# Second layer of a two-layer model on one core: the inverse roots of eight norms by Newton steps on VectorE, with the layer's four written orders made anew

## What is computed

```
x = x + L1_attn_a(layernorm(x))   # a linear layer, sigmoid and tanh, a linear scan over the tokens
x = x + L1_ffn(layernorm(x))      # silu(h @ up) * (h @ gate) @ down, ternary weights, 1024 wide
x = x + L1_attn_b(layernorm(x))   # rmsnorm, a gated linear recurrence (RG-LRU), rmsnorm, a gelu MLP 768 wide
x = x + L1_ffn(layernorm(x))      # the same feed-forward block again
```

## Time and profile before

| | |
|---|---|
| median of 3 runs | 1489.52 us (1486.73 to 1493.4) |
| the profiled execution | 1492.75 us, of which the span from the first to the last instruction is 1491.5 us |
| PE busy | 1424.5 us, 96% of the span |
| DVE, ACT, POOL busy | 1078.2, 1045.0, 678.5 us |
| second layer | 1224.5 to 1491.5 us of the span, 267 us |
| ACT_TABLE_LOAD in the second layer | 42, of 1283 ns each |

### The profile page before, as it was taken

How to read it: one execution, slowest core, us unless ns; L and a number is a source line. 1 busy time by engine, 2 the same in 40 slices (tenths; PEclk the granted TensorE clock), 3 DMA queues, 4 the chain that set the end, 5 groups by cost and what they waited for, 6 DMA issues and landing times.

```text
span 1491.5 us, 23534 instructions
## 1 busy us (share of the span) xinstructions
PE 1424.5 (96%) x8388; PEld 1215.6 (81%) x8388; DVE 1078.2 (72%) x2439; ACT 1045.0 (70%) x2281; POOL 678.5 (45%) x822
## 2 busy tenths in 40 slices
PE   7899999999999998998999999999999998979899
PEld 6789898888989886786898888888897786656677
DVE  6989898989898985656776666666676748567534
ACT  4898989999898987474665555655564646584754
POOL 6676776676767546113433343333321111822223
PEclk9999999999999999898999999999999999998999
DMA  2000000000000000601000000000001404000000
GB/s 74 2 18 1 19 9 12 1 19 19 1 8 2 15 1 1 268 1 51 22 15 15 22 23 14 22 22 22 1 8 63 207 28 171 1 1 1 1 0 29
DMA packets 14339, 45.11 MB, mean 30 GB/s; under 512 B 3216, under 2 KB 3216, under 8 KB 12048
## 3 DMA queue, kind: packets, MB, share of 16 engines
q1 hardware_dynamic: 14224, 43.61, 8.1%
HBM read 42.55 MB, written 1.05 MB: 29 GB/s over the span
## 4 chain that ended last, share of the span: by engine, by line
PE 75%; DVE 15%; ACT 7%; issue 1%; POOL 1%; DVEq 0%; ACTq 0%; POOLq 0%
PE ps L149 32%; PE ps L355 15%; PE ps L344 10%; PE ps L1198 6%; DVE a_pT_lo L411 3%; PE ps L2007 3%; PE ps L2013 2%; DVE a_prob L364 2%; DVE a_q L694 1%; PE ps L2023 1%; PE ps L2009 1%; PE ps L2026 1%; PE ps L1910 1%; PE ps L614 1%; ACT a_prob L371 1%
## 5 line engine op out<-in xcount | busy, mean ns | idle before, releaser
L386 POOL TENSOR_SCALAR a_prob<-a_prob,a_rowinv 128x128 f32<-128x128 f32 (+7 forms) x256 | 188.2, 749 | 132.8 <-DVE a_rowinv L380 132.7
L411 DVE TENSOR_TENSOR a_pT_lo<-ps,a_pT_hi 128x512 fp32r<-128x512 f32 (+3 forms) x384 | 194.7, 551 | 21.1 <-ACT a_pT_hi L403 19.4
L364 DVE CUSTOM_DVE_ANT_0 a_prob<-ps,a_mask 128x128 f32<-128x128 f32 (+7 forms) x256 | 187.1, 750 | 21.2 <-PE ps L149 20.9
L371 ACT ACTIVATE a_prob<-a_prob,a_negmax 128x128 f32<-128x128 f32 (+7 forms) x256 | 197.3, 778 | 2.2 <-DVE a_negmax L364 1.3
L386 POOL TENSOR_SCALAR b_prob<-b_prob,b_rowinv 128x128 f32<-128x128 f32 (+7 forms) x128 | 94.3, 748 | 199.9 <-DVE b_rowinv L380 199.8
L403 ACT ACTIVATE a_pT_hi<-ps 128x512 fp32r<-128x512 f32 (+3 forms) x384 | 167.2, 492 | 24.7 <-PE ps L344 15.6
L344 PE MATMUL ps<-ident,a_prob 128*128 128x128 f32 x1152 | 160.2, 275 | 7.1 <-DVE a_pT_lo L411 5.7
L371 ACT ACTIVATE b_prob<-b_prob,b_negmax 128x128 f32<-128x128 f32 (+7 forms) x128 | 99.6, 779 | 72.6 <-DVE b_negmax L364 71.8
L344 PEld LDWEIGHTS ps<-ident,a_prob 128*128 128x128 f32 x1152 | 130.0, 140 | 20.6 <-POOL a_prob L386 8.0
L149 PE MATMUL ps<-a_k_hi,a_q 128*128 128x512 f32 (+3 forms) x384 | 140.4, 373 | 1.8 <-DVE a_negmax L364 1.2
L355 PE MATMUL ps<-a_pT_hi,a_v 128*128 128x512 f32 (+3 forms) x384 | 131.1, 349 | 1.1 <-DVE a_pT_lo L411 0.6
(11 more groups left out here) (457 smaller groups left out, 4024.0 us busy)
## 6 DMA issues: line engine op xcount, KB each, us to landing
f_wq<-in_f_wq SPq DMA_DIRECT2D x2, 2048.0 KB, 8.9
f_wo<-in_f_wo SPq DMA_DIRECT2D x2, 2048.0 KB, 17.1
b_w_raw<-in_b_qk SPq DMA_DIRECT2D x16, 256.0 KB, 2.6
a_w_raw<-in_a_w SPq DMA_DIRECT2D x8, 384.0 KB, 3.2
a_vo<-in_a_o SPq DMA_DIRECT2D x8, 256.0 KB, 2.7
f_wk<-in_f_wk SPq DMA_DIRECT2D x2, 1024.0 KB, 10.8
f_wv<-in_f_wv SPq DMA_DIRECT2D x2, 1024.0 KB, 12.8
f_wg<-in_f_wg SPq DMA_DIRECT2D x2, 1024.0 KB, 19.7
```

Source lines behind the costliest of these rows:

```text
L364: dve.tensor_tensor_reduce(slot(a, u), g.ps_flat[:, bank * HALF:bank * HALF + width], a.mask[:, N - width:], -1.0, -MASKED, ALU.add, ALU.m ...
L371: act.activation(prob, prob, ACT.Exp, bias=a.negmax[:, n:n + 1], scale=-1.0, accum_out=a.rowsum[:, n:n + 1]).then_inc(*g.exped.mark(a.tag, u))
L386: pool.tensor_scalar(prob, prob, a.rowinv[:, n:n + 1], 1.0, ALU.mult, ALU.mult).then_inc(*g.normed.mark(a.tag, u))
L411: dve.tensor_tensor(lo, src, fr(hi), ALU.subtract).then_inc(*g.lo.mark(a.tag, u, j0 // 4))
```

## The change

Three things change, all in the second layer.

1. **ACT loses its root in eight norms** (r, t1, n2, t2 of both halves): `half_root_act` is no longer called there, and with it go the 128x4 ACTIVATE and the table loads around it. The listing of ACT's order has 32 ACT_TABLE_LOAD in the layer now, 42 before.
2. **DVE computes the inverse root itself**, from the variance in PSUM: add eps, shift the bits right by one, subtract them from a constant (a first guess), and three Newton steps of three instructions each, `half_inverse_dve`. That is 12 instructions on 128x4 values in place of one reciprocal. Each waits for the one before it by a semaphore. The product inside a Newton step is kept in PSUM, in four unused columns of `q.bank[1]`.
3. **All four order strings are new.** The steps are the same ones (ACT has eight fewer), in another interleaving of prep, half 0 and half 1.

```diff
+ROOT_BITS, ROOT_STEPS = float(0x5F375A00), 3
+I32 = mybir.dt.int32
 L1_PE = (
-    "12112201201112122110211121211111112111112111112211121222122112211112222211112222211221121112122122122112222111111122"
...
+    "12112012101112210221211112111121111111111111221111222212121211122221222111122222211122121112122222211122212111111112"
...
-def half_inverse_dve(g, dve, q, tag):
-    dve.wait_ge(*q.act.at(tag, "std"))
-    dve.reciprocal(q.inv[:], q.std[:]).then_inc(*q.dve.mark(tag, "rec"))
+def half_inverse_dve(g, dve, q, tag, eps):
+
+    done, part = q.dve, q.bank[1][:, HT:2 * HT]
+    dve.wait_ge(*q.pe.at(tag, "var"))
+    dve.tensor_scalar(q.std[:], q.bank[1][:, 0:HT], eps, None, ALU.add).then_inc(*done.mark(tag, "plus"))
+    dve.wait_ge(*done.at(tag, "plus"))
+    dve.tensor_scalar(q.inv[:].bitcast(I32), q.std[:].bitcast(I32), 1, None, ALU.logical_shift_right).then_inc(*done.mark(tag, "half_bits"))
+    dve.wait_ge(*done.at(tag, "half_bits"))
+    dve.tensor_scalar(q.inv[:].bitcast(I32), q.inv[:].bitcast(I32), -1.0, ROOT_BITS, ALU.mult, ALU.add).then_inc(*done.mark(tag, "step", 0))
+    for n in range(ROOT_STEPS):
+        dve.wait_ge(*done.at(tag, "step", n))
+        dve.tensor_tensor(part, q.inv[:], q.inv[:], ALU.mult).then_inc(*done.mark(tag, "part", n))
+        dve.wait_ge(*done.at(tag, "part", n))
+        dve.scalar_tensor_tensor(part, part, -0.5, q.std[:], ALU.mult, ALU.mult).then_inc(*done.mark(tag, "slope", n))
+        dve.wait_ge(*done.at(tag, "slope", n))
+        event = (tag, "rec") if n == ROOT_STEPS - 1 else (tag, "step", n + 1)
+        dve.scalar_tensor_tensor(q.inv[:], part, 1.5, q.inv[:], ALU.add, ALU.mult).then_inc(*done.mark(*event))
     yield
...
-def half_norm_act(g, act, q, tag, eps):
+def half_norm_act(g, act, q, tag):
     yield from half_square_act(g, act, q, tag, q.h, "cen")
-    yield from half_root_act(g, act, q, tag, eps)
     yield from half_hi_act(act, q, tag, q.h, "out")
...
     yield from half_square_act(g, act, q, "n2", q.u, "x1")
-    yield from half_root_act(g, act, q, "n2", 1e-8)
     yield from half_hi_act(act, q, "n2", q.h, "out")
```

More of the change, by code:

```diff
@@ L1688 @@
 RING = 3
+ROOT_BITS, ROOT_STEPS = float(0x5F375A00), 3
+I32 = mybir.dt.int32
 L1_PE = (
[L1690 to L1691 removed]
+    "12112012101112210221211112111121111111111111221111222212121211122221222111122222211122121112122222211122212111111112"
+    "21212122222222122221221121122212111111211111211122122122222222222222222111222")
 L1_DVE = (
[L1693 to L1694 removed]
+    "01112212112101000002121202110010102201121120012012112210011221111211211121111111121212111111121111121121122111122212"
+    "22222222212222112222122222222121211222222111221211111222212212112122221222221122211222")
 L1_ACT = (
[L1696 to L1697 removed]
+    "11220110111122112020221112211111111011221111212211112211221222211121111111211221121111222222112221122211222221122211"
+    "221222222112222211122211112211111112122112222222221222222")
 L1_POOL = (
[L1699 removed]
+    "0110101011010022222201112011212111222222211111112222222")
 def by_turns(order, *programs):
@@ L1988, in half_norm_dve @@
     yield from half_squares_dve(dve, q, tag)
-    yield from half_inverse_dve(g, dve, q, tag)
+    yield from half_inverse_dve(g, dve, q, tag, 1e-5)
     dve.wait_ge(*q.pe.at(tag, "inv"))
@@ L2110, in half_act @@
 def half_act(g, l, act, q):
-    yield from half_norm_act(g, act, q, "r", 1e-5)
+    yield from half_norm_act(g, act, q, "r")
     for n, m in enumerate((0, 2, 1, 3)):
@@ L2127, in half_ternary_act @@
 def half_ternary_act(g, l, act, q, tag):
-    yield from half_norm_act(g, act, q, tag, 1e-5)
+    yield from half_norm_act(g, act, q, tag)
     for f in range(TE_T):
@@ L2294, in half_lru_dve @@
     yield from half_squares_dve(dve, q, "n2")
-    yield from half_inverse_dve(g, dve, q, "n2")
+    yield from half_inverse_dve(g, dve, q, "n2", 1e-8)
     dve.wait_ge(*pe.at("n2", "inv"))
```

6 lines of the change are left out of this document (removed).

## The result

The changed kernel takes **1500.88 us** in the median of 5 runs (1496.38 to 1506.11) against 1489.52 us for the kernel before: a ratio of 1.0073, 95% interval 1.0055 to 1.0091. It is 11 us slower. The forecast was 1498 us, with 1483 to 1505 as its range.

The account below looks back on a forecast made before the run. The prediction took PE, busy 96% of the span, to bound the kernel. Stretch terms 0.5 + 0 + 7.0 + 1.7 - 0.7 = +8.5 gave 1501.2 us profiled, less 3.2 for the median: 1498 us, range 1483 to 1505.

Parts of the forecast that it names:

- The turns: DVE and POOL alternate by operation; five SBUF-only instructions of the twelve each wait up to one POOL operation; 9.3 us.
- The walk through n2 of half 0: Fourth stretch: remainder, sum of squares, shift and subtraction wait for POOL's operations in turn; +7.7 us, taken as +7.0.
- the longer chain: n2 of half 0: twelve dependent DVE instructions delay the spread even without turns, 5.75 instead of 3.9 us, +1.9.
- The order terms: First two stretches: new interleaving costs +2.0 us in the first; the second, with its other terms, is taken as -3.8.
- The second stretch: To half 0's l mean: moved blocks, less idle and slow clock, against turns in t1 of half 1; -3.8 us taken.
- The third stretch: To the end of half 0's `out`: the silu cut goes (3.3 us), ga starts some 3 us later; 0, give or take 2.
- The fifth stretch: To half 1's n2 spread: order nearly the same, 2.35 us chain faces one 1.4 us down block, adds come behind; +1.7 us.
- The sixth stretch: To the end: blocks of 4.7 to 5.6 us cover the chain in t2's norms; tail stays; -0.7 us.
- The last step: From the profiled 1501.2 us to the median: subtract 3.2 us, as the profiled execution before stood over its median; 1498.
- the turns don't bite: Rival, no change: four elements too few for the second port, or splits fall elsewhere; 9.3 us go, 1489; chance 0.27.
- ScalarE's relief decides: Rival, faster: removed ACT table loads and the uncut ga free more than the rows name; -8.4 us, 1481; chance 0.17.
- the clock decides: Rival, slower: longer norm in n2 of half 0 starves PE and lowers its clock; 1501 to 1507 us; chance 0.13.

Follow-up runs that it names:

- e4: Changed kernel with the same twelve instructions, but variance plus eps and shifted bits kept in PSUM, so none reads SBUF alone: 1490.11 us, ratio 1.0000.
- e10: Changed kernel with POOL's two long weight-remainder subtractions cut, r_lo into four pieces and down_lo into six, same work: 1497.62 us, ratio 1.0057.
- e3: Changed kernel with POOL's split of the down weights and half 1's last remainder moved ahead of both adds to x: 1502.09 us, ratio 1.0078.
- e6: e4's chain in PSUM with the order strings of the kernel before: 1503.82 us, ratio 1.0095.
- e12: e4 with the old order on all four engines from half 0's l mean to its n2 spread (third and fourth stretch): 1493.76 us, ratio 1.0020.
- e1: Kernel before with the four new order strings, keeping ScalarE's root and its eight steps: 1494.80 us, ratio 1.0026.
- e2: Changed kernel (Newton root on DVE, chain in SBUF) with the four old order strings, less ScalarE's eight root steps: 1508.77 us, ratio 1.0128.

## Why the prediction was right, step by step

| stretch | forecast | measured |
|---|---|---|
| 1, to t1's first block | +4.3 | +3.7 |
| 2, to half 0's l mean | -3.8 | -3.8 |
| 3, to the end of `out` | 0 | -0.6 |
| 4, to the spread of n2, half 0 | +7.0 | +7.9 |
| 5, to the spread of n2, half 1 | +1.7 | +3.2 |
| 6, to the end | -0.7 | -1.9 |
| sum | +8.5 | +8.5 |

**The turns** are shown, by e4 (taken away), e10 (their size changed) and e3 (moved). In r of half 0 one instruction took 2.08 us, where about 2.2 was expected; in n2 of half 0 the gap between variance and spread is 6.65 us, where 5 or more was to prove the turns. In the sum they were 2.3 + 1.9 + 5.1 = 9.3 us; taking those of the twelve away is worth 10.8 in the median and 8.4 in the stretches. The Trainium skill (SBUF — State Buffer, Who interferes with whom) says that a VectorE instruction with two SBUF inputs, or in a two-port mode, blocks against a POOL operation that reads SBUF, and that one with at most one SBUF input outside those modes does not. The runs agree for the squarings, which wait in the changed kernel, and for e4, where none of the twelve waits. Shift and subtraction have one SBUF input and wait as well; that they ran in a two-port mode is not shown, since the profile does not name the mode. That the shift and the subtraction on 128x4 count, which the prediction had left open, is shown by their 2.08 and 3.32 us.

**The walk through n2 of half 0** came out at 12.9 us against a forecast of 12.0 (5.0 + 7.0), but not by its own steps. The remainder did not wait for POOL (0.68 us at 1347.65), and the shift ran free (0.17), since the long split began only 0.04 us after it. The subtraction waited for the long split and the squaring for the add, one place later each than I wrote.

Its terms were off by more than its result. I had 1.9 us for the longer chain and 5.1 for turns, and nothing for the order. The table splits the 7.9 otherwise. From e4 to the changed kernel it is 3.2, the turns of the twelve; with the turn of the sum of squares, which e4 keeps (1.57 us in place of 0.69), it is 4.1. The other 4.7 (9.7 less 5.0) are there without any turn in the chain. By e6, which has the long chain in the old order and reads 6.9, 1.9 of them are the chain and 2.8 the order, which I had left out: it puts the two down rounds behind the variance, PE's wait of 3.11 us for the sum of squares has nothing to cover it, and what follows runs at half clock. How chain and order share the 4.7 is not settled, since e12, whose order there is e6's, reads 8.2 at a granted clock of 0.87 where e6 has 0.99. That the turns fell short of my term and the rest went over it by about as much is luck.

**The order terms.** In the first stretch I had 2.3 for the turn in r and 2.0 for the order, a walk. PE's wait for that spread gives the turn: 2.18 us in the changed kernel, 0.26 in e4.

```profile
1232.58 1.16 PE L249 MATMUL ps<-ident,l_inv 128*128 128x128 f32 x8 [2.18 <-DVE l_inv L1985]
```

```profile
1233.03 1.16 PE L249 MATMUL ps<-ident,l_inv 128*128 128x128 f32 x8 [0.26 <-DVE l_inv L1985]
```

That leaves 1.8 of the +3.7 for the order and the longer chain, and e4's first stretch is 1.7 over before (42.3 less 40.6), within the 2 us that such a stretch varies. e1's +3.6 does not speak against it: it has no chain, but PE waits 2.75 us for x ahead of a mean there, against 0.80 in the changed kernel. The second stretch came out at the forecast; e4 gives its turns 1.5 us (32.2 to 30.7) against the 1.9 of the sum.

**The third stretch** was where I expected trouble, with two effects that cancel. PE waits 1.52 us for `ga` and 5.80 us later, where before it waited 8.50 us and 1.70 for `out`; the cut by half 1's silu is gone, and the copies come late:

```profile
1324.04 0.47 PE L2022 MATMUL ps<-l_h_hi,l_ga_hi 128*128 128x512 f32 x1 [1.52 <-ACT l_h_hi L1952]
...
1338.58 1.22 PE L2022 MATMUL ps<-l_h_hi,l_t_up 128*128 128x512 f32 x2 [5.80 <-ACT l_work L2146]
```

**The fifth stretch was too small by 1.5 us**, and for a reason that the sum lacked. I wrote that the order there is nearly the same. It isn't on POOL, whose string now puts the two products of half 1's recurrence between half 0's remainders. The second remainder stands behind a product that waits 17.00 us for ScalarE, and PE waits for that remainder. POOL and PE of the changed kernel:

```profile
1391.16 1.26 POOL L2335 TENSOR_TENSOR l_work<-l_work,l_h 128x512 f32<-128x512 f32 x1 [17.00 <-ACT l_work L2169]
1392.38 1.26 POOL L2348 TENSOR_TENSOR l_ring_lo<-l_work,l_ring_hi 128x512 fp32r<-128x512 f32 x1
```

```profile
1393.70 0.50 PE L2038 MATMUL ps<-l_ring_hi,l_down_hi 128*128 128x512 f32 x1 [2.54 <-POOL l_ring_lo L2348]
```

The wait is in e1 and e4 too (2.54 and 2.55) and not in before or e6, so it comes with the order; in return the 3.59 us that before waits for a gelu in this stretch fall to 0.83. e6, which has the chain and the old order, is 2.6 longer than before, e1, which has the new order and no chain, 4.4. So either alone costs more than my term of 1.7, or as much within what one execution tells, and together they cost 3.2: the two are not a sum, and how they share it stays open.

**The sixth stretch** was -1.9 where I had -0.7. The fifth missed by +1.5 and the sixth by -1.2, so that the sum came out at the forecast is partly luck.

**The last step**, from the profiled execution to the median, is where the 3 us of difference between 1498 and 1500.88 come from. I subtracted 3.2 us, since the profiled execution of before stood that much over its median. That of after stood 2.1 us below its median of runs, and its first layer was 2.4 us shorter than that of before: 3.2 + 2.1 - 2.4 = 2.9. One execution against five is no offset to carry over. It also means that the +8.5 of the stretches is one execution against another, while the medians differ by 11.4; the 2.9 between them are not placed.

**The rivals.** That the turns don't bite is refuted by e4, whose 1490.1 is also what that rival gave (1489). That ScalarE's relief decides: e4 has all of the relief and none of the turns, and is level with before, not 8 us under it. That the clock decides: by the six rows the changed kernel spends 24 us of the layer at 1.2 GHz, the kernel before 28; it has more of them than before in the first, fourth and fifth stretch (7, 5 and 5 us against 4, 0 and 3), less in the second and third. In the fourth the clock is a part of the loss, but e4 is lower there still (0.65) and 3.2 us faster. In e2 and e6 the clock is part of the loss (49 and 41 us at 1.2 GHz), behind the waits of the spreads.
